# Statistics, banks and closing additions moved in a two-layer graph and mixture-of-experts kernel

## The chip, the cores and the metric

The kernel runs on one core of a Trainium2 chip. The metric is the time of one execution on the device in microseconds; the number that counts is the median of repeated runs. All arithmetic is fp32.

## What is computed

The reference takes 8192 tokens of 128 features (32 graphs of 256 nodes) and passes them through four blocks, each normalised before and added back to the tokens after.

```python
x = x + gated_graph(layernorm(x), adj)      # layer 0: (adj @ x + bias) * gates, relu
x = x + top1_experts(layernorm(x))          # H = gelu(x @ W1 + b1); x = p_e * (H @ Wd[e] + bd[e])
x = x + graph_lstm(layernorm(x), adj)       # layer 1, below
x = x + top2_experts(layernorm(x))          # y_e = (silu(x @ w1_e) * (x @ w3_e)) @ w2_e
```

The third block is

```python
h = relu(einsum('ts,bsh->bth', adj, x @ Wg0 + bg0))
h = relu(einsum('ts,bsh->bth', adj, h @ Wg1 + bg1))
for p in 1..4:                              # windows of p nodes, an LSTM over each
    h[:, last node of each window] = lstm_p(windows of h)
```

## The kernel before

Every engine has its own program, and semaphores tie them. A tile is 128 tokens; there are 64 tiles, held in `X` in on-chip memory through the whole kernel. The order of work on each engine is written out by hand. The stages that matter here are these.

**First experts, b2.** Tokens are sorted by expert into 72 slots, taken four at a time in 18 groups (`NB2`). On TensorE a group is `b2_pe` (hidden products, line 1150, and expert products, line 1291); ScalarE does the gelu; on VectorE `b2_dve` (from line 2016) adds the bias and leaves the result (line 2027), and SyncE stores it. GpSimd gathers the results back in token order (`gather`, line 689) in three runs: tiles 0 to 23, 24 to 31, and 32 to 63. In groups 13 to 16 VectorE also adds eight gathered tiles per group to `X` and takes their statistics (`b3_tile`, line 1991). After group 16 it finishes mean and reciprocal deviation of tiles 0 to 31 together (`b3_finish`, `ln_finish`, lines 1513 to 1532), and at the start of group 17 it normalises the first two groups of four tiles (`g_norm`, line 2006), ahead of the bias of group 17.

**Graph, c1, twice (halves of 32 tiles, eight groups of four).** TensorE per group: `g_mix` (line 1331, into bank 0), `g_hidden` (line 1340), `g_second` (line 1348), `g_out` (line 1359, into bank 3). ScalarE copies the mix out of its bank (`g_mixed`, line 917), and the next mix waits for that copy since both use bank 0. VectorE adds the bias (`g_bias0`, line 2052) and normalises the groups ahead. In the second half, transposes of the first half's result are mixed in (line 1302).

**LSTM, twice.** TensorE lines 1415 and 1422. VectorE adds gathered tiles 32 to 63 during the first one.

**Second experts, d2.** 136 slots (`8 * ND2`), one at a time, in groups of eight. Per slot i: TensorE does the upper products of i (line 1442) and then the lower ones of i - 2 (line 1452, `d2_down`, banks 6 and 7 in turn); ScalarE does silu (line 1032) and copies weights (line 955); VectorE multiplies (line 2243) and scales the result of slot i - 2 into `yd` (`d2_rows_out`, line 2172); GpSimd sends the rows home with an indirect DMA (`rows_home`, line 710). The home rows come back in ten blocks (`D3_BLOCKS`): blocks 0 to 5 of eight tiles, 6 to 9 of four. SyncE loads blocks 0 to 3 (`d3_load(0)`), then 4 and 5 once four additions are done (`d3_load(1)`), stores 0 to 3, stores 4 and 5, and only then loads 6 to 9, for which all rows must be home (line 545), and stores them. Each block needs two additions on VectorE (`d3_add`, line 2193, one per expert). Eight are made within the slots, at those given by `D3_ADDS` counted back from the end (slots 119, 121, ... 133); the four of blocks 4 and 5 and the eight of blocks 6 to 9 follow behind the last slot.

```python
D3_ADDS = (17, 15, 13, 11, 9, 7, 5, 3)
for i in [*D3_OF[1], *D3_OF[2]]:
    for k in range(2):
        d3_add(i, k)
```

Of the kernel before, what the change touches and what calls it, by code (L numbers as in the profile page):

```python
# [5 lines left out]
P = 128  # L6
# [49 lines left out]
def build(nc, x, adj_t, bias_io, gate_w, gate_b, w1, b1, wg, bg, wd, bd, g0_w, g0_b, g1_w, g1_b, wih_t, whh_t, bih, bhh,  # L56
# [4 lines left out]
    MC = N // P  # L61
# [25 lines left out]
    with ExitStack() as ctx:  # L87
# [229 lines left out]
        b3_x, b3_t = sem("b3_x"), sem("b3_t")  # L317
# [34 lines left out]
        D3_ADDS = (17, 15, 13, 11, 9, 7, 5, 3)  # L352
# [229 lines left out]
        def _(pool):  # L582
# [133 lines left out]
            for lo, hi, done in GATHERS:  # L716
                gather(lo, hi, done)
            def t_finish(half, k, n):
                first = half * NGH + n * k
                pool.wait_ge(t_ln, first + n)  # L720
                ln_finish(4 * first, 4 * (first + n), half > 0, t_rstd)
# [28 lines left out]
        def _(act):  # L750
# [166 lines left out]
            def g_mixed(half, i):  # L917
                n = half * NGH + i
                act.wait_ge(c1_ax, n + 1)
                if n >= 2:  # L920
                    act.wait_ge(c1_h, n - 1)
                act.activation(axt[i % 2], bank[0][:, :], ACT.Copy).then_inc(c1_axc, 1)
# [133 lines left out]
        def _(pe):  # L1056
# [267 lines left out]
            def g_mix(half, i):  # L1324
                n = half * NGH + i
                pe.wait_ge(c1_xn, n + 1)
                if n > 0:
                    pe.wait_ge(c1_axc, n)
                for b in range(2):
                    for m in range(MC):  # L1330
                        mm = pe.matmul(bank[0][:, b * N:(b + 1) * N], xn[i % 2][:, MC * b + m, :], adj_sb[:, m, :],  # L1331
# [115 lines left out]
            def d2_down(i, j, expert, straight):  # L1447
# [3 lines left out]
                for c in range(KU):  # L1451
                    mm = pe.matmul(bank[6 + j % 2][:, 0:D], hm[j % 2][0:HC, c * P:(c + 1) * P],  # L1452
# [51 lines left out]
            for j in (6, 7):  # L1504
                d2_down(8 * (ND2 - 1) + j, j, er[j - 6], False)
# [3 lines left out]
        def _(dve):  # L1509
# [491 lines left out]
            def b3_finish(half):  # L2001
                dve.wait_ge(b3_t, (half + 1) * NH)
                ln_finish(half * NH, (half + 1) * NH)


            def g_norm(half, i):
                n = half * NGH + i
                if n >= 2:
                    dve.wait_ge(c1_ax, n - 1)
                for j in range(4):  # L2010
# [5 lines left out]
            def b2_dve(g, k, u, first, last):  # L2016
                if isinstance(g, int) and g == NB2 - 1:
                    g_norm(0, 0)
                    g_norm(0, 1)
# [15 lines left out]
                if ahead_of_end == 2:  # L2035
                    b3_finish(0)
# [88 lines left out]
            for half in range(HALVES):  # L2125
# [25 lines left out]
                for n in range(NL):  # L2151
# [11 lines left out]
                    if half == 0 and n == NL - 3:  # L2163
                        b3_finish(1)


            def d2_rows_out(i):
                g, j = i // 8, i % 8
                dve.wait_ge(d2_y, i + 1)
                if j == 0 and g >= RING:  # L2170
                    dve.wait_ge(d2_out[g % RING], 128 * (g // RING))
                dve.tensor_scalar(yd[g % RING][:, j, :], bank[6 + j % 2][:, 0:D], slot_gate[:, i:i + 1], None,  # L2172
# [92 lines left out]
            for i in [*D3_OF[1], *D3_OF[2]]:  # L2265
# [46 lines left out]
```

## Time and profile before

| | us |
|---|---|
| median of 3 runs | 1147.16 |
| lowest, highest | 1145.66, 1150.82 |
| the profiled execution's own time | 1153.07 |
| its span | 1151.2 |
| TensorE busy in the span | 1024.0 (89%) |
| VectorE busy | 600.0 (52%) |
| ScalarE busy | 619.4 (54%) |
| GpSimd busy | 483.7 (42%) |
| mean granted TensorE clock | 0.956 of full |

The span runs from the first to the last record of one execution; 1.9 us of the execution's own time lie around it. In the rows below the engines are PE (TensorE products), PEld (its weight loads), DVE (VectorE), ACT (ScalarE), POOL (GpSimd) and SP (SyncE, whose queue is SPq). L12 is line 12 of the kernel. An fp32 product is recorded as two passes, so one mix of four products shows as x8. The chain of waits is followed back from the last instruction to what released it.

### The profile page before, as it was taken

The numbers are of one execution on the slowest core, as the hardware profiler recorded it, in microseconds if no ns is written. First come the engines' busy times: TensorE is split into PE (matmuls) and PEld (weight loads), VectorE is DVE, ScalarE is ACT, GpSimd is POOL, SyncE is SP. The second block draws the span as 40 slices with busy tenths as digits, with TensorE's granted clock in tenths as the row PEclk, the third lists the DMA queues.
The fourth block names the chain that finished last, engine by engine and source line by source line (L and its number), as shares of the span: only waits on it lengthen the run. The fifth ranks groups of instructions, "written<-read, shape, count | busy, mean of one in ns | idle before, by whom it ended". The sixth has DMA issues, their size and how long they took to land.

```text
span 1151.2 us, 17554 instructions
## 1 busy us (share of the span) xinstructions
PE 1024.0 (89%) x5432; PEld 715.8 (62%) x5433; DVE 600.0 (52%) x1829; ACT 619.4 (54%) x1158; POOL 483.7 (42%) x703
## 2 busy tenths in 40 slices
PE   5799967899989899999999996999897799989993
PEld 2344423577667544654785463448897798889893
DVE  6977874411174265655756753336464523333365
ACT  4678843444333485655338754456776555545551
POOL 5852274531634420000220075533536666656652
PEclk9899988799998999999999997999998999999997
DMA  9940012232323030000000011121122222212547
GB/s 274 365 193 1 1 50 69 87 97 70 97 71 86 28 116 0 1 1 0 1 1 1 1 48 40 41 61 31 43 62 65 64 81 65 82 62 66 189 164 223
DMA packets 79876, 86.28 MB, mean 75 GB/s; under 512 B 10115, under 2 KB 65971, under 8 KB 79027
## 3 DMA queue, kind: packets, MB, share of 16 engines
q1 hardware_dynamic: 67250, 59.28, 16.2%
q0 software_dynamic: 12544, 25.98, 6.8%
q8 instruction: 44, 0.72, 0.3%
q14 instruction: 38, 0.30, 0.1%
HBM read 40.64 MB, written 44.58 MB: 74 GB/s over the span
## 4 chain that ended last, share of the span: by engine, by line
PE 67%; DVE 13%; ACT 6%; issue 6%; another core or an unknown queue 6%; DMA 1%; ACTq 1%; POOL 1%; DVEq 0%; POOLq 0%; SPq 0%
PE bank L1415 17%; PE bank L1442 14%; PE bank L1422 9%; PE bank L1452 5%; PE bank L1150 4%; PE bank L1291 3%; PE bank L1331 2%; PE bank L1179 2%; PE bank L1359 2%; ACT sb_whh_sb L955 1%; PE bank L1348 1%; PE bank L1320 1%; PE bank L1340 1%; DVE sb_R L1542 1%
## 5 line engine op out<-in xcount | busy, mean ns | idle before, releaser
L1415 PE MATMUL bank<-sb_R,sb_wih_sb 128*128 128x512 f32 (+2 forms) x504 | 203.0, 554 | 15.0 <-ACT sb_R L975 7.6
L975 ACT ACTIVATE sb_R<-bank,sb_lb_sb 128x512 f32<-128x512 f32 (+2 forms) x252 | 153.2, 634 | 93.4 <-PE bank L1422 67.4
L710 POOL DMA_INDIRECT expert_out<-sb_R,sb_slot_row x136 | 132.6, 975 | 115.9 <-ACT sb_R L998 45.5
L2243 DVE TENSOR_TENSOR sb_R<-sb_R,bank 114x384 f32<-114x384 f32 x136 | 75.3, 554 | 181.9 <-ACT sb_R L1032 107.3
L1415 PEld LDWEIGHTS bank<-sb_R,sb_wih_sb 128*128 128x128 f32 x504 | 97.1, 194 | 113.7 <-issue 82.8
L1032 ACT ACTIVATE sb_R<-bank 114x384 f32<-114x384 f32 x136 | 66.4, 489 | 142.5 <-PE bank L1442 102.8
L1442 PE MATMUL bank<-sb_xt,sb_wih_sb 128*114 128x128 f32 x792 | 103.5, 282 | 22.8 <-issue 7.2
L1452 PE MATMUL bank<-sb_BIG,sb_R 114*128 x816 | 115.7, 278 | 0.7 <-DVE sb_R L2172 0.5
L1442 PEld LDWEIGHTS bank<-sb_xt,sb_wih_sb 128*114 128x114 f32 x792 | 94.1, 184 | 28.6 <-issue 25.4
L1422 PE MATMUL bank<-sb_R,sb_whh_sb 128*128 128x512 f32 (+2 forms) x288 | 111.1, 529 | 0.0
L685 POOL DMA_INDIRECT expert_in<-sb_R,sb_dest_i x64 | 64.4, 1007 | 105.1 <-DVE sb_dest_i L1767 62.7
L1452 PEld LDWEIGHTS bank<-sb_BIG,sb_R 114*128 114x128 f32 x816 | 103.5, 194 | 0.9 <-issue 0.9
L1442 PE MATMUL bank<-sb_xt,sb_whh_sb 128*114 128x128 f32 x792 | 98.6, 274 | 5.7 <-ACT sb_wih_sb L955 5.6
L614 POOL TENSOR_TENSOR sb_ln_p<-sb_ST 128x8 f32<-128x8 f32 (+2 forms) x15 | 3.3, 222 | 222.6 <-DVE sb_ST L1657 162.5
L1442 PEld LDWEIGHTS bank<-sb_xt,sb_whh_sb 128*114 128x114 f32 x792 | 91.2, 178 | 8.1 <-issue 7.1
L899 ACT ACTIVATE sb_R<-bank,sb_b_sb 128x512 f32<-128x512 f32 x72 | 47.9, 688 | 83.9 <-PE bank L1150 75.0
L1422 PEld LDWEIGHTS bank<-sb_R,sb_whh_sb 128*128 128x128 f32 x288 | 54.7, 190 | 50.5 <-issue 35.6
L676 POOL DMA_INDIRECT sorted_in<-sb_R,sb_dest_i x64 | 62.9, 983 | 44.2 <-issue 16.9
L729 POOL DMA_INDIRECT expert_in<-sb_R,sb_dest_i x64 | 61.9, 967 | 41.1 <-PE bank L1442 16.2
L1291 PE MATMUL bank<-sb_BIG,sb_R 128*128 x576 | 69.8, 279 | 8.3 <-issue 4.3
L1179 PE MATMUL bank<-sb_xt,sb_w_sb 128*128 128x512 f32 x128 | 68.5, 632 | 9.1 <-ACT sb_R L828 9.1
L1291 PEld LDWEIGHTS bank<-sb_BIG,sb_R 128*128 128x128 f32 x576 | 67.6, 195 | 9.4 <-issue 9.4
(308 smaller groups left out, 1690.9 us busy)
## 6 DMA issues: line engine op xcount, KB each, us to landing
sb_XS<-expert_in SPq DMA_DIRECT2D x17, 528.0 KB
expert_in<-sb_R SPq DMA_DIRECT2D x17, 512.0 KB, 6.1
sb_R<-expert_out SPq DMA_DIRECT2D x6, 1024.0 KB, 8.3
sorted_in<-sb_R SPq DMA_DIRECT2D x9, 512.0 KB, 5.4
sb_XS<-sorted_in SPq DMA_DIRECT2D x18, 256.0 KB
sorted_out<-sb_R SPq DMA_DIRECT2D x18, 256.0 KB
sb_X<-x SPq DMA_DIRECT2D x8, 512.0 KB, 7.4
out<-sb_X SPq DMA_DIRECT2D x6, 512.0 KB
```

Source lines behind the costliest of these rows:

```text
L676: pool.indirect_dma_start(out=sorted_in, out_offset=bass.IndirectOffsetOnAxis(ap=dest_i[:, 0, t:t + 1], axis=0), in_=XN[:, t, :], in_offse ...
L685: pool.indirect_dma_start(out=expert_in, out_offset=bass.IndirectOffsetOnAxis(ap=dest_i[:, k, t:t + 1], axis=0), in_=XR[:, t, :], in_offse ...
L710: pool.indirect_dma_start(out=expert_out, out_offset=bass.IndirectOffsetOnAxis(ap=slot_row[:, i:i + 1], axis=0), in_=yd[i // 8 % RING][:, ...
L975: act.activation(gb[s][k][:, 0:c], bank[4 * s + k][:, 0:c], funcs[k], bias=lb_sb[:, (p - 1) * GATES + k:(p - 1) * GATES + k + 1]).then_inc ...
L1032: act.activation(sl[j % 2][0:HC, :], bank[2 + 2 * (j % 2)][0:HC, 0:KU * P], ACT.Silu).then_inc(d2_silu, 1)
L1179: pe.matmul(bank[2 + c % 2][:, :], w1_sb[:, c * P:(c + 1) * P], xt[b // 2 % 2][:, b % 2 * BANK:(b % 2 + 1) * BANK], start=True, stop=True) ...
L1291: mm = pe.matmul(bank[6 + u][:, j * P:(j + 1) * P], Ht[u][:, c, j * P:(j + 1) * P], wd_sb[:, c, bass.ds(er[j] * D, D)], start=(c == 0 and ...
L1415: mm = pe.matmul(bank[4 * s + k][:, 0:c].rearrange("p (w b) -> p w b", b=GH), wih_sb[:, p - 1, k * P:(k + 1) * P], xin, start=True, stop=( ...
L1422: pe.matmul(bank[4 * s + k][:, 0:c], whh_sb[:, p - 1, k * P:(k + 1) * P], hst[s][:, 0:c], start=False, stop=True).then_inc(l_g, 1)
L1442: mm = pe.matmul(bank[2 + 2 * (j % 2) + part][0:HC, c * P:(c + 1) * P], weights_of(i)[:, part * UP + c * HC:part * UP + (c + 1) * HC], xt[ ...
L1452: mm = pe.matmul(bank[6 + j % 2][:, 0:D], hm[j % 2][0:HC, c * P:(c + 1) * P], down_sb[0:HC, bass.ds(expert * (KU * D) + c * D, D)], start= ...
L2243: dve.tensor_tensor(hm[j % 2][0:HC, :], sl[j % 2][0:HC, :], bank[3 + 2 * (j % 2)][0:HC, 0:KU * P], ALU.mult).then_inc(d2_m, 1)
```

## The change

Four edits. (1) In b2, VectorE finishes the statistics of tiles 0 to 23 after group 15 instead of those of 0 to 31 after group 16, and normalises the first two groups there, ahead of the bias of group 16. (2) The statistics of tiles 24 to 31 are finished by GpSimd, between its second and third run of gathers; the normalisation of the seventh group waits for them. (3) The second mix of each half goes into bank 3 and waits for no copy. (4) `D3_ADDS` holds twelve places, slots 117, 118, 120, 121, 123, 124, 126, 127, 129, 130, 132 and 133, so that only the eight additions of blocks 6 to 9 stand behind the last slot; and the last slot's lower product goes into bank 0 and doesn't wait for the result of slot 133 to be read.

```diff
-        b3_x, b3_t = sem("b3_x"), sem("b3_t")
+        b3_x, b3_t, b3_rstd = sem("b3_x"), sem("b3_t"), sem("b3_rstd")
+        SOON = 3 * NH // 4
+        def mix_bank(i):
+            return bank[3] if i == 1 else bank[0]
-        D3_ADDS = (17, 15, 13, 11, 9, 7, 5, 3)
+        D3_ADDS = (19, 18, 16, 15, 13, 12, 10, 9, 7, 6, 4, 3)
             for lo, hi, done in GATHERS:
                 gather(lo, hi, done)
+                if hi == NH:
+                    pool.wait_ge(b3_t, NH)
+                    ln_finish(SOON, NH, False, b3_rstd)
-                act.activation(axt[i % 2], bank[0][:, :], ACT.Copy).then_inc(c1_axc, 1)
+                act.activation(axt[i % 2], mix_bank(i)[:, :], ACT.Copy).then_inc(c1_axc, 1)
-                if n > 0:
+                if n > 0 and i != 1:
                     pe.wait_ge(c1_axc, n)
-                        mm = pe.matmul(bank[0][:, b * N:(b + 1) * N], xn[i % 2][:, MC * b + m, :], adj_sb[:, m, :],
+                        mm = pe.matmul(mix_bank(i)[:, b * N:(b + 1) * N], xn[i % 2][:, MC * b + m, :], adj_sb[:, m, :],
-            for j in (6, 7):
-                d2_down(8 * (ND2 - 1) + j, j, er[j - 6], False)
+            d2_down(8 * ND2 - 2, 6, er[0], False)
+            d2_down(8 * ND2 - 1, 7, er[1], True, bank[0])
+                if half == 0 and 4 * i == SOON:
+                    dve.wait_ge(b3_rstd, 1)
-                if isinstance(g, int) and g == NB2 - 1:
-                    g_norm(0, 0)
-                    g_norm(0, 1)
-                if ahead_of_end == 2:
-                    b3_finish(0)
+                if ahead_of_end == 3:
+                    dve.wait_ge(b3_t, SOON)
+                    ln_finish(0, SOON)
+                    g_norm(0, 0)
+                    g_norm(0, 1)
-            for i in [*D3_OF[1], *D3_OF[2]]:
+            for i in D3_OF[2]:
                 for k in range(2):
                     d3_add(i, k)
```

## Rows read from the trace of the kernel before

**Rows 1.** The profile's chain of waits, its share of the span by engine

```profile
PE 67%; DVE 13%; ACT 6%; issue 6%; another core or an unknown queue 6%; DMA 1%; ACTq 1%; POOL 1%; DVEq 0%; POOLq 0%; SPq 0%
```

**Rows 2.** Timeline, first graph opening: start, us, engine, line, operation, [idle before it]

```profile
336.88 0.89 DVE L2027 TENSOR_TENSOR sb_R<-bank,sb_BIG 128x128 f32<-128x128 f32 x4
...
341.95 0.22 DVE L1517 TENSOR_TENSOR sb_ln_t<-sb_ST 128x32 f32<-128x32 f32 x1
...
345.33 2.14 DVE L2012 TENSOR_SCALAR sb_xn<-sb_X,sb_MEAN,sb_RSTD 128x128 f32<-128x128 f32 x8
...
346.50 3.08 PE L1331 MATMUL bank<-sb_adj_sb,sb_xn 128*128 128x256 f32 x8 [3.06 <-DVE sb_xn L2012]
347.38 0.89 DVE L2027 TENSOR_TENSOR sb_R<-bank,sb_BIG 128x128 f32<-128x128 f32 x4
...
350.41 3.75 PE L1331 MATMUL bank<-sb_adj_sb,sb_xn 128*128 128x256 f32 x8 [0.84 <-ACT sb_R L922]
...
354.94 1.97 PE L1331 MATMUL bank<-sb_adj_sb,sb_xn 128*128 128x256 f32 x8
```

**Rows 3.** Windows, PE only: stretch, its length, busy (count), granted clock, DMA share

```profile
347.00:347.50 0.50, 0.50 (x3) 0.75 0.00 0
```

**Rows 4.** Timeline and windows, all engines, in b2: an idle TensorE and the clock

```profile
332.60 3.83 PE L1291 MATMUL bank<-sb_BIG,sb_R 128*128 x32 [1.49 <-ACT sb_R L899]
...
330.00:345.00 15.00, 11.94 (x78) 9.24 (x76) 12.47 (x56) 5.66 (x9) 0.67 (x1) 1.00 0.16 45
```

**Rows 5.** Timeline, second graph opening, and one window of PE there

```profile
547.05 1.89 PE L1331 MATMUL bank<-sb_adj_sb,sb_xn 128*128 128x256 f32 x8
...
548.52 1.11 DVE L2012 TENSOR_SCALAR sb_xn<-sb_X,sb_MEAN,sb_RSTD 128x128 f32<-128x128 f32 x4
...
551.00 2.73 PE L1331 MATMUL bank<-sb_adj_sb,sb_xn 128*128 128x256 f32 x8 [2.06 <-ACT sb_R L922]
...
555.48 0.69 DVE L2052 TENSOR_TENSOR sb_R<-bank,sb_bga_sb 128x512 f32<-128x512 f32 x1 [4.22 <-PE bank L1340]
...
552.50:553.00 0.50, 0.50 (x2) 0.50 0.00 0
```

**Rows 6.** Timeline behind the last slot, then two pieces of the chain there

```profile
1132.41 4.87 DVE L2200 TENSOR_TENSOR sb_X<-sb_R,sb_X 128x1024 f32<-128x1024 f32 x4
1132.93 1.53 POOL L710 DMA_INDIRECT expert_out<-sb_R,sb_slot_row  x1 [0.30 <-issue]
...
1143.05 5.40 DVE L2200 TENSOR_TENSOR sb_X<-sb_R,sb_X 128x512 f32<-128x512 f32 x8 [5.77 <-DMA sb_R<-expert_out]
...
1134.76 3.64 DMA expert_out<-sb_R,sb_slot_row
...
1138.65 4.38 DMA sb_R<-expert_out
```

**Rows 7.** Timeline, POOL: first and last of nine statements finishing eight tiles' statistics

```profile
568.51 0.23 POOL L614 TENSOR_TENSOR sb_ln_p<-sb_ST 128x8 f32<-128x8 f32 x1 [5.60 <-DVE sb_ST L1657]
...
570.78 1.67 POOL L623 TENSOR_TENSOR sb_RSTD<-sb_ln_p,sb_minus_half 128x8 f32<-128x8 f32 x1
```

**Rows 8.** Timeline: an addition on DVE and the POOL issue that starts inside it

```profile
1118.72 1.22 DVE L2200 TENSOR_TENSOR sb_X<-sb_R,sb_X 128x1024 f32<-128x1024 f32 x1
...
1119.56 1.21 POOL L710 DMA_INDIRECT expert_out<-sb_R,sb_slot_row  x1 [1.07 <-PE bank L1442]
```

**Rows 9.** Loads of home rows (timeline; landing by the profile's DMA issues), and slot 118

```profile
1082.51 1.94 SPq L556 DMA_DIRECT2D sb_R<-expert_out  x4
...
sb_R<-expert_out SPq DMA_DIRECT2D x6, 1024.0 KB, 8.3
...
1093.32 0.55 DVE L2243 TENSOR_TENSOR sb_R<-sb_R,bank 114x384 f32<-114x384 f32 x1 [1.38 <-remote]
```

**Rows 10.** Timeline: a last indirect DMA with queues quiet, and SP's load released by it

```profile
769.16 0.96 POOL L685 DMA_INDIRECT expert_in<-sb_R,sb_dest_i  x1 [0.30 <-issue]
...
771.45 272.51 SPq L537 DMA_DIRECT2D sb_XS<-expert_in  x15
```

More of the change, by code:

```diff
@@ L1445, in d2_up, with d2_down @@
                 mm.then_inc(d2_h, 1)
-            def d2_down(i, j, expert, straight):
+            def d2_down(i, j, expert, straight, target=None):
+                target = target or bank[6 + j % 2]
                 pe.wait_ge(d2_m, i + 1)
@@ L1451, in d2_down @@
                 for c in range(KU):
-                    mm = pe.matmul(bank[6 + j % 2][:, 0:D], hm[j % 2][0:HC, c * P:(c + 1) * P],
+                    mm = pe.matmul(target[:, 0:D], hm[j % 2][0:HC, c * P:(c + 1) * P],
                                    down_sb[0:HC, bass.ds(expert * (KU * D) + c * D, D)],
@@ L1999, in b3_tile, with b3_finish @@
                         dve.bn_stats(ST[:, q, :], X[:, q, :]).then_inc(b3_t, 1)
-            def b3_finish(half):
-                dve.wait_ge(b3_t, (half + 1) * NH)
-                ln_finish(half * NH, (half + 1) * NH)
+            def b3_finish():
+                dve.wait_ge(b3_t, 2 * NH)
+                ln_finish(NH, 2 * NH)
             def g_norm(half, i):
@@ L2163, in _ @@
                     if half == 0 and n == NL - 3:
-                        b3_finish(1)
+                        b3_finish()
             def d2_rows_out(i):
                 g, j = i // 8, i % 8
+                source = bank[0] if i == 8 * ND2 - 1 else bank[6 + j % 2]
                 dve.wait_ge(d2_y, i + 1)
@@ L2171, in d2_rows_out @@
                     dve.wait_ge(d2_out[g % RING], 128 * (g // RING))
-                dve.tensor_scalar(yd[g % RING][:, j, :], bank[6 + j % 2][:, 0:D], slot_gate[:, i:i + 1], None,
+                dve.tensor_scalar(yd[g % RING][:, j, :], source[:, 0:D], slot_gate[:, i:i + 1], None,
                                   ALU.mult).then_inc(d2_yo, 1)
```

## The prediction

> **What bounds the kernel now.** I read the chain of waits first, to see which engine's time is the kernel's time: TensorE holds 67% of it [rows 1]. So an edit pays only where TensorE waits, or behind its last product. Then I read the timeline at the three places that the change touches.
>
> In the first graph opening TensorE ends the last expert product at 343.44 (346.50 less 3.06 idle) and waits for VectorE, which finishes the statistics from 341.95 to 345.33 and then normalises. The first two mixes take 3.08 and 3.75 us where the third takes 1.97 [rows 2]. The reason is the granted clock: it goes from full to half, 2.4 to 1.2 GHz, inside the window at 347.0 to 347.5, after TensorE had stood idle for 3.06 us [rows 3]. An idle of 1.49 us in the group before left the clock at 1.00 [rows 4]. In the second opening the first mix ends at 548.94 and the second starts at 551.00, after the copy out of bank 0; it takes 2.73 us, and the window at 552.5 shows 0.50 [rows 5]. Behind the last slot the chain goes through GpSimd's last row transfer (3.64 us to landing), the first load of home rows (4.38) and eight additions (5.40) [rows 6].
>
> **The change part by part.**
>
> **Statistics a group sooner.** VectorE's work is only put in another order. From 336.88: statistics 3.38 us (341.95 to 345.33) and two normalisations of 2.05 (345.33 to 347.38), so the first normalised group is there at 341.3 and the second at 342.3, both before TensorE ends at 343.44. The bias of group 16 slips from 336.88 to 342.3; its eight tiles (4.18 us, from 337.77 to 341.95) end at 347.4, and the bias of group 17 starts at 347.4 as before [rows 2]. Narrower statistics (24 columns for 32) may give back 0.1 us. TensorE then mixes at full clock: 343.5 to 345.4, the second until 347.3, the first hidden product (354.16 to 354.94 in [rows 2], 0.8 us) until 348.1. The third mix needs the third normalisation, which stands behind group 17's bias: 347.4 + 0.9 + 1.1 = 349.4. Before it started at 354.94. Gain 5.5 us; what is late next is this third normalisation, with an idle of 1.3 us before it, shorter than the 1.49 of [rows 4] that left the clock alone.
> Moved with it: the store of group 16's result on SyncE goes 5.4 us later, but the third run of gathers needs the store of group 17, which doesn't move. The expert product of group 17 needs only the bias of group 15. I put both at nothing.
>
> **Last eight tiles by GpSimd.** Nine statements, 568.51 to 572.45, so 3.9 us [rows 7]. They start once the tiles are added (347.4) and end at 351.3. Behind them on GpSimd stand the 32 gathers of tiles 32 to 63, each of which also waits for a hidden product (the first at 348.1) and for the last store. They lose at most 3.2 us, and their readers are in the LSTM after eight graph groups. The seventh normalisation waits for the fifth mix, thus until after 349.5 + 3 x 1.9 = 355.2; the cover is 3.9 us. Cost nothing; without that cover TensorE would wait for the rest.
>
> **Second mix in its own bank.** In the first half it is worth nothing, since the third mix waits for VectorE anyway: with the copy's 0.84 us of wait [rows 2] the hidden product would end at 348.9, still before 349.4. In the second half the second mix is held only by its normalisation, which ends at 549.63. It runs until 551.5, the hidden product until 552.3, and VectorE's bias, at 555.48 before, starts at 552.4 [rows 5]. That is 2.06 - 0.7 of wait and the rest half clock: TensorE's idle shrinks to 0.7 us. Gain 3.1. Bank 3 is next written by the first output product, two rounds later, behind the copy.
>
> **Twelve additions within the slots.** An addition of 1.22 us [rows 8] is put where VectorE waits 1.38 us, as before slot 118's product [rows 9]; two slots in three take one, where before one in two did. A slot lasts 2.3 us (slot 118's product at 1093.32, slot 129's addition at 1118.72, [rows 8, 9]), and VectorE's own work in one is 0.55 us of product and a scaling that I take as no longer, so 2.3 with an addition. Behind an addition a product can slip a little, and the slot without one takes it up. TensorE wants the product only two slots later: nothing, bounds -0.5 and +1.5 us, since GpSimd and VectorE may each be held by the other once. The first addition wants block 0 at 1091.9 (1093.32 - 1.38); the load was issued at 1082.51 and takes 8.3, so it is there at 1090.8 [rows 9]. Loads 4 and 5 and all stores of 0 to 5 go out some 9 us earlier on SyncE, since the fourth addition comes at slot 121 instead of 125.
> Behind the last slot four additions of 1.22 us vanish, but not from the end: they run from 1132.41 to 1137.28, and the loads of blocks 6 to 9 wait until 1138.4 for the last rows [rows 6]. What goes is what they did to others. (a) An indirect DMA issued inside an addition is held: it starts at 1119.56, the addition ends at 1119.94, it ends at 1120.77, 0.83 us later [rows 8]. The same sum gives the 1.53 us at 1132.93 (addition ends 1133.63). Without it 0.96: gain 0.57. (b) Two stores of 512 KB stand before the last transfer: 3.64 us to landing, against 2.29 with quiet queues (769.16 to 771.45) [rows 6, 10]: gain 1.35, bounds 0 and 1.35. (c) The first load shares the queues with the end of the last store: between 0 and 2.1 (4.38 less 2.29); I take 0.7, half of what a block of that size takes (5.40 over 4) [rows 6, 10]. The eight last additions stay. Together 2.6, bounds 0 and 4.0.
> The Trainium skill ("SBUF — State Buffer", section "Who interferes with whom") says that a VectorE instruction with two inputs on chip blocks a GpSimd instruction that reads there, not one that only writes, and infers that tensor_tensor therefore doesn't hold descriptor generation. By that rule term (a) is nothing and the sum 0.6 us smaller; the trace disagrees, with 1.21 and 1.53 against 0.96, and I go by the trace.
>
> **The last slot's bank.** GpSimd issues rows one after another (0.96 and 0.30 between), and the last was issued at 1134.76 while its rows were scaled before the additions began at 1132.41 [rows 6]. The queue is GpSimd's: nothing.
>
> **Sum.** 5.5 + 3.1 + 2.6 = 11.2 us. The profiled execution took 1153.07 (span 1151.2 and 1.9 around it), so its like would take 1141.9. It stands 5.9 above the median; from the median 1147.16 - 11.2 = 1136.0.
>
> **The rivals.**
> *The tail gives nothing:* landing is bound by the transfer and not by its company, and the loads take what they took. For it: one quiet landing is thin evidence. 1136.0 + 2.6 = 1138.6. A case within it, with 0.04 of its chance: the row issue is slow for another reason than the addition, so only (a) fails: 1136.6. The rule of the Trainium skill above would give this.
> *The clock falls in the first opening all the same.* TensorE is idle for 1.3 us where 2.06 and 3.06 came before a fall and 1.49 didn't. The first two mixes took 6.8 us together where two at full clock take 3.8 [rows 2]; of these 3.0 us 1.3 would lie in the idle: 1136.0 + 1.7 = 1137.7.
> *Both openings fall to half clock and the tail gives nothing:* 1.7 in the first, 1.8 in the second (551.00 to 555.48 is 4.5 us for a mix and a hidden product that take 1.9 and 0.8 [rows 5]): 11.2 - 2.6 - 3.5 = 5.1, thus 1142.1, within 0.5%.
> *Slower:* the additions wait for their blocks. Place: slot 117, where block 0 has 1.1 us to spare by 8.3 us of landing. VectorE stands still, then TensorE, since the upper product of slot i needs the multiplied slot i - 2. It decides once VectorE waits over 11.2 us in all at these twelve places, and passes 0.5% at 17; block 4, loaded at slot 121 and wanted at 129, has 8 x 2.3 - 8.3 = 10 us to spare on top, so a single late block doesn't do it. With 18 us of waiting 1154. Against it: before, the only wait in front of an addition is the 5.77 us behind the last slot [rows 6].
>
> **How the numbers follow.** A measurement of this kernel can tell about 0.5% (5.7 us) from no change. Chances: forecast 0.52, tail nothing 0.16, clock in the first opening 0.14, both 0.12, slower 0.04, and 0.02 for something that gives all back. Faster 0.82, same 0.14, slower 0.04. The forecast's own bounds are 1134.5 (tail 4.0) to 1138; with the scatter of the median (1.5 below, 3.7 above in three runs) and the case of both falls the range is 1132.0 to 1142.5.
>
> **What would show it.** The first mix starts right behind the last expert product, with no idle before it, and the third about 6 us after it; granted clock 1.00 in both openings; nine GpSimd statements between gathers; the second mix of the second half starts 0.7 us after the first ends; no 1.53 us row issue behind the last slot; about 2.3 us from the last issue to the loads; no VectorE idle before its additions in the slots. A half clock in an opening, an idle at slot 117, or a landing of 3.6 us would show the step that failed.

## The result and the profile after

Six runs of each kernel on one chip: 1146.37 us before (1145.66 to 1150.82), 1139.64 after (1137.37 to 1141.25), ratio 0.9931 with an interval of 0.9916 to 0.9945. By the ratio that is 7.9 us less (6.3 to 9.6). The two medians themselves lie 6.7 us apart, inside that interval; ratio and median are two estimates from the same runs, and every "us less" below goes by the ratio. The forecast was 1136.0 with a range of 1132.0 to 1142.5 and "faster" at 0.82: sign and range hold, and the measured time is 3.6 us longer than forecast. One run of the kernel before on the second chip below (1237.6 us) and one of e5_fill there (2109.5 us) stand far above all others and are in no ratio. The profiled pair differs by more than the medians: 1153.07 against 1141.25, 11.8 us (spans 1151.2 and 1139.5). That is close to the forecast sum of 11.2. Why a pair of profiles shows the sum and the medians don't is the main question below.

The timeline of the kernel after, first opening, beside [rows 2] (start, us, engine, line, operation, [idle before it]):

```profile
343.14 0.87 DVE L2034 TENSOR_TENSOR sb_R<-bank,sb_BIG 128x128 f32<-128x128 f32 x4
...
344.33 3.62 PE L1338 MATMUL bank<-sb_adj_sb,sb_xn 128*128 128x256 f32 x16
...
347.66 1.08 ACT L929 ACTIVATE sb_R<-bank 128x512 f32<-128x512 f32 x2 [6.02 <-DVE sb_X L2002]
...
348.24 0.21 POOL L618 TENSOR_TENSOR sb_ln_p<-sb_ST 128x8 f32<-128x8 f32 x1 [16.52 <-DVE sb_ST L2007]
348.26 0.88 DVE L2034 TENSOR_TENSOR sb_R<-bank,sb_BIG 128x128 f32<-128x128 f32 x4
...
348.31 1.12 PE L1347 MATMUL bank<-sb_R,sb_g_sb 128*128 128x512 f32 x2 [0.37 <-ACT sb_R L929]
...
349.06 1.10 DVE L2022 TENSOR_SCALAR sb_xn<-sb_X,sb_MEAN,sb_RSTD 128x128 f32<-128x128 f32 x4
...
350.21 1.99 PE L1338 MATMUL bank<-sb_adj_sb,sb_xn 128*128 128x256 f32 x8 [0.78 <-DVE sb_xn L2022]
...
350.38 1.67 POOL L627 TENSOR_TENSOR sb_RSTD<-sb_ln_p,sb_minus_half 128x8 f32<-128x8 f32 x1
...
352.71 1.08 POOL L708 DMA_INDIRECT sb_R<-sorted_out,sb_dest_i  x1 [0.59 <-POOL sb_pause_p L663]
```

The reader is to see three things. The sixteen products of the first two mixes stand as one group of 3.62 us with no idle before it, where before there were 3.08 and 3.75 us after 3.06 of idle. The third mix comes 5.9 us after the last expert product (344.33 to 350.21) where it came 11.5 after (343.44 to 354.94), and its idle of 0.78 us is VectorE's third normalisation, behind the bias of group 17. And one line that the prediction doesn't have: ScalarE's first copy of a mix starts at 347.66, 1.4 us after the first mix ends (344.33 and 1.89 us for a mix), released by VectorE's sums (L2002) and not by TensorE. GpSimd's nine statements run from 348.24 to 352.05; the gather behind them starts at 352.71.

The second opening, beside [rows 5]:

```profile
543.67 1.89 PE L1338 MATMUL bank<-sb_adj_sb,sb_xn 128*128 128x256 f32 x8
...
546.28 1.99 PE L1338 MATMUL bank<-sb_adj_sb,sb_xn 128*128 128x256 f32 x8 [0.72 <-DVE sb_xn L2022]
...
549.17 0.69 DVE L2062 TENSOR_TENSOR sb_R<-bank,sb_bga_sb 128x512 f32<-128x512 f32 x1 [1.32 <-PE bank L1347]
...
549.87 1.89 PE L1338 MATMUL bank<-sb_adj_sb,sb_xn 128*128 128x256 f32 x8
```

The idle is 0.72 us for 2.06, the mix takes 1.99 us for 2.73, and from the first mix to the third it is 6.2 us. Before, the third mix started at 556.24, 9.19 us after the first.

The granted clock over the two openings, from the first mix to the third (stretch, length, busy of PE, PEld, DVE, ACT, POOL, clock, DMA share, GB/s):

```profile
344.30:350.30 6.00, 4.86 (x21) 3.26 (x19) 5.75 (x24) 1.08 (x2) 1.69 (x8) 1.00 0.19 53
543.60:549.90 6.30, 5.58 (x28) 4.26 (x27) 4.95 (x14) 2.61 (x6) 0.00 (x0) 1.00 0.00 0
```

It is full (2.4 GHz) in both, where [rows 3] and [rows 5] have 0.75 and 0.50.

Behind the first opening the kernel after gives some of this back, at a place that the prediction doesn't look at:

```profile
365.61 1.06 ACT L940 ACTIVATE sb_R<-bank 128x512 f32<-128x512 f32 x1 [4.08 <-remote]
...
367.14 1.16 PE L1355 MATMUL bank<-sb_g_sb,sb_R 128*128 128x128 f32 x8 [1.04 <-ACT sb_R L936]
```

ScalarE waits 4.08 us for something that the profile can't name ("remote"), and TensorE then waits 1.04 us for ScalarE. The sixth and the seventh mix start 6.5 us apart, where they are 5.2 us apart in the kernel before.

In the slots and behind the last one, beside [rows 6, 8], first the timeline, then two pieces of the chain:

```profile
1083.40 1.22 DVE L2211 TENSOR_TENSOR sb_X<-sb_R,sb_X 128x1024 f32<-128x1024 f32 x1
...
1083.46 1.98 POOL L714 DMA_INDIRECT expert_out<-sb_R,sb_slot_row  x1 [0.30 <-issue]
...
1115.68 1.22 DVE L2211 TENSOR_TENSOR sb_X<-sb_R,sb_X 128x1024 f32<-128x1024 f32 x1
...
1116.52 1.20 POOL L714 DMA_INDIRECT expert_out<-sb_R,sb_slot_row  x1 [0.92 <-PE bank L1449]
...
1123.72 0.96 POOL L714 DMA_INDIRECT expert_out<-sb_R,sb_slot_row  x1 [0.31 <-issue]
...
1131.42 5.40 DVE L2211 TENSOR_TENSOR sb_X<-sb_R,sb_X 128x512 f32<-128x512 f32 x8 [8.50 <-DMA sb_R<-expert_out]
...
1124.98 2.22 DMA expert_out<-sb_R,sb_slot_row
...
1127.45 3.94 DMA sb_R<-expert_out
```

The last row issue but one takes 0.96 us where it took 1.53, the last rows land in 2.22 where it was 3.64, the first load takes 3.94 where it was 4.38: 0.57 + 1.42 + 0.44 = 2.4 us. The additions now stand inside the slots, none of the twelve with an idle before it. Each row issue that starts inside one ends 0.82 to 0.84 us after it (1084.62 and 1085.44, 1116.90 and 1117.72), so these issues take 1.01 to 1.98 us. An issue that had started before the addition isn't held: it takes 0.95 or 0.96 us, as outside.

One line of the kernel before belongs beside the landing, how long SyncE itself waited for it (us in total, times, longest):

```profile
SPq L545 <- DMA expert_out<-sb_R,sb_slot_row: 0.7, 1, 0.7
```

SyncE came to this wait only 0.7 us before the rows had landed, since it stood in the store of block 5, which waits for the fourth addition. So a sooner landing alone would have been worth 0.7 us at most; it is worth 1.42 because the additions moved, and SyncE's wait for them with them.

### The profile page after: what moved, and what is told of

Same layout as the page of the kernel before. It is cut to its first block, busy times and chain, and to the rows that moved or that the text cites. A ratio compares the mean times of both kernels' runs of the same rounds, so it can differ in the third digit from the quotient of the medians.

```text
span 1139.5 us, 17561 instructions
## 1 busy us (share of the span) xinstructions
PE 1016.3 (89%) x5432; PEld 712.0 (62%) x5433; DVE 599.0 (53%) x1829; ACT 618.5 (54%) x1158; POOL 489.1 (43%) x712
## 4 chain that ended last, share of the span: by engine, by line
PE 67%; DVE 13%; another core or an unknown queue 7%; ACT 6%; issue 4%; ACTq 1%; DMA 1%; POOL 0%; DVEq 0%; POOLq 0%; SPq 0%
PE bank L1422 16%; PE bank L1449 15%; PE bank L1429 9%; PE bank L1460 5%; PE bank L1157 4%; PE bank L1298 4%; PE bank L1186 2%; PE bank L1366 2%; ACT sb_whh_sb L962 1%; PE bank L1338 1%; ACTq L956 1%; PE bank L1327 1%; PE bank L1355 1%; DVE sb_R L1550 1%
## 5 line engine op out<-in xcount | busy, mean ns | idle before, releaser
L1422 PE MATMUL bank<-sb_R,sb_wih_sb 128*128 128x512 f32 (+2 forms) x504 | 200.2, 548 | 14.5 <-ACT sb_R L982 10.6
```

The lines of the kernel that those rows point to most:

```text
L1422: mm = pe.matmul(bank[4 * s + k][:, 0:c].rearrange("p (w b) -> p w b", b=GH), wih_sb[:, p - 1, k * P:(k + 1) * P], xin, start=True, stop=( ...
```

## The experiments

They ran on two other chips than the pair above. On the second one the kernel before takes 1158.3 and 1158.7 us in two series (27 runs between 1150.5 and 1162.7; 27 between 1150.1 and 1162.1). On the third it takes 1063.7 (9 runs, 1061.5 to 1064.3). Microseconds behind a ratio are the ratio times the median of before there.

To compare the traces I measure five stretches in each:

- O1, the first opening: from the end of the last expert product (the first mix's start less its idle) to the third mix of the first half;
- R, the rest of that half: from its third mix to the first mix of the second half;
- O2, the second opening: from the first mix to the third of the second half;
- D, in the expert slots: from the first to the last upper product whose weights lie in `sb_wih_sb`. Slots take `sb_wih_sb` and `sb_whh_sb` in turn, two slots each, so this last product is not that of the last slot, which comes 3.9 us later;
- T, the tail: from the end of D to the end of the span.

In brackets: the edits of this stretch that the kernel has ("part" is the statistics without GpSimd).

```
                 chip    O1 us          R us            O2 us          D us    T us
before           first   11.5           192.1           9.2            335.2   26.1
after            first    5.9 (all)     193.5 (stats)   6.2 (bank)     335.7   23.6 (adds)
e1_stats         second   6.9 (stats)   193.3 (stats)   9.2            340.4   26.2
e2_bank          second  10.6 (bank)    192.6           6.2 (bank)     342.4   26.0
e3_adds          second   8.6           192.6           9.2            339.4   23.7 (adds)
e5_fill          second   8.8 (fill)    192.2           7.5 (fill)     340.7   25.8
e6_whole         second   5.9 (all)     193.7 (stats)   6.2 (bank)     338.9   23.6 (adds)
e8_third         second   4.4 (all)     196.0 (stats)   6.2 (bank)     340.3   23.7 (adds)
e9_dve           second   9.4 (part)    194.6 (part)    6.2 (bank)     340.1   23.6 (adds)
e10_order        second  10.0           192.6           7.5            339.2   27.5 (order)
e4_same          third   11.2           192.1           7.5            290.1   26.0
e12_same         third   10.0           192.1           7.5            290.1   25.8
e15_half1        third    5.5 (stats)   192.1 (stats)   6.2 (bank)     290.1   23.6 (adds)
e14_last         third    4.4 (all)     192.1 (stats)   6.2 (bank)     290.1   23.7 (adds)
```

R holds what O1 alone would hide. On the third chip it is 192.1 us whatever the kernel. On the first two it is 192.1 to 192.6 with the old order of the statistics and 193.3 to 196.0 with the new one, so about 1 us of the gain in the first opening is given back there, and more in e8_third and e9_dve. In e6_whole and e1_stats it goes where it went in the kernel after, between the sixth and the seventh mix (6.7 and 6.4 us apart). GpSimd's eight tiles aren't the cause, since e9_dve has none of them and an R of 194.6; what ScalarE and VectorE wait for there stays open.

Between the openings and the slots, from the third mix of the second half to the first product of D, lies a stretch that no kernel here edits. It takes 225.3 to 233.7 us on the first two chips and 214.5 to 214.6 on the third. So single executions on the first two chips can differ there by more than the whole change is worth.

### The three parts alone: e1_stats, e2_bank, e3_adds

e1_stats is the kernel before with the order of VectorE's statistics and GpSimd's last eight tiles changed, and no other edit.

```diff
-                if ahead_of_end == 2:
-                    b3_finish(0)
+                if ahead_of_end == 3:
+                    dve.wait_ge(b3_t, SOON)
+                    ln_finish(0, SOON)
+                    g_norm(0, 0)
+                    g_norm(0, 1)
...
```

> Only the statistics are moved (tiles 0 to 23 a group sooner, the last eight tiles on GpSimd). Theory A (the forecast's terms hold in every execution): 5.5 us faster than before, ratio 0.9952, and no half clock in the first opening. Theory B (the profiled execution of before lost more in its openings and slots than its timed runs do, so each term is worth less in timed runs): 2 to 4 us, ratio 0.9965 to 0.998. In the profile of either the third mix starts some 6 us after the last expert product ends.

Measured: 1153.99 us, ratio 0.9947 (0.9926 to 0.9968), 6.1 us less (3.7 to 8.6), as theory A had it. O1 is 6.9 us, not some 6. Its timeline there:

```profile
346.16 1.89 PE L1335 MATMUL bank<-sb_adj_sb,sb_xn 128*128 128x256 f32 x8
...
350.26 1.97 PE L1335 MATMUL bank<-sb_adj_sb,sb_xn 128*128 128x256 f32 x8 [2.21 <-ACT sb_R L926]
```

The second mix waits 2.21 us for ScalarE's copy out of bank 0, not the 0.84 of [rows 2]. That copy stands behind ScalarE's wait for all 32 sums of the first half, which in the kernel before had long been met, and now has not. So in the first half the second bank isn't worth nothing once the statistics are sooner: it takes 1.0 us more off (6.9 to 5.9).

e2_bank is the kernel before with the second mix of each half in bank 3.

```diff
-                if n > 0:
+                if n > 0 and i != 1:
                     pe.wait_ge(c1_axc, n)
-                        mm = pe.matmul(bank[0][:, b * N:(b + 1) * N], ...
+                        mm = pe.matmul(bank[3 if i == 1 else 0][:, b * N:(b + 1) * N], ...
...
```

> Only the second mix gets its own bank. In the first opening the second mix then follows the first without the copy's 0.84 us, still behind the late statistics. Theory A: 3.1 us in the second opening and up to 1 us in the first, together 3 to 4 us, ratio 0.9965 to 0.997. Theory B: 1.5 to 2.5 us, only the idle without the clock.

Measured: 1153.99 us, 0.9965 (0.9942 to 0.9988), 4.1 us less (1.4 to 6.7), again theory A's figure. In the trace O2 is 6.2, as forecast. In O1 the clock fell as in the kernel before:

```profile
348.44 6.76 PE L1331 MATMUL bank<-sb_adj_sb,sb_xn 128*128 128x256 f32 x16 [3.05 <-DVE sb_xn L2012]
```

Two mixes in 6.76 us; alone they take 3.62 at full clock in the kernel after.

e3_adds moves the twelve additions and nothing else.

```diff
-        D3_ADDS = (17, 15, 13, 11, 9, 7, 5, 3)
+        D3_ADDS = (19, 18, 16, 15, 13, 12, 10, 9, 7, 6, 4, 3)
-            for i in [*D3_OF[1], *D3_OF[2]]:
+            for i in D3_OF[2]:
```

> Only the twelve additions within the slots. Theory A: 2.6 us from the tail, ratio 0.9977, landing of the last rows 2.3 us instead of 3.64 in the profile. Theory B: the tail gives the same 2.5 us but the denser additions cost 1 to 3 us in the slots, so the ratio is 0.999 to 1.0.

Measured: 1155.09 us, 0.9968 (0.9943 to 0.9993), 3.7 us less (0.8 to 6.6), over theory A's 2.6 and against theory B. T is 23.7, 2.4 below the kernel before. But this trace has more in it, in a place that it doesn't edit, the first opening:

```profile
348.01 1.99 PE L1331 MATMUL bank<-sb_adj_sb,sb_xn 128*128 128x256 f32 x8 [3.06 <-DVE sb_xn L2012]
...
350.84 1.97 PE L1331 MATMUL bank<-sb_adj_sb,sb_xn 128*128 128x256 f32 x8 [0.84 <-ACT sb_R L922]
...
346.00:348.00 2.00, 0.00 (x0) 0.00 (x0) 1.86 (x9) 0.00 (x0) 0.00 (x0) 1.00 0.00 0
348.00:350.00 2.00, 1.99 (x8) 1.44 (x8) 1.78 (x8) 0.00 (x0) 0.00 (x0) 1.00 0.00 0
350.00:352.00 2.00, 1.16 (x7) 1.06 (x7) 1.12 (x4) 0.60 (x1) 0.00 (x0) 1.00 0.49 127
```

The same code, the same idle of 3.06 us to the hundredth, and the clock stays at 1.00: 1.99 and 1.97 us for mixes that took 3.08 and 3.75 in [rows 2]. So a fall after this idle is something that happens in some executions and not in others.

### Filling the idle: e5_fill

The kernel before, with products that nobody reads in TensorE's two idles, into bank 2, which is free there; each is 128x512 and stands as two records.

```diff
+                if (half, i) == (0, 0):
+                    fill(3)
+                if (half, i) == (1, 1):
+                    fill(2)
...
```

> The kernel before, with TensorE kept busy by idle products into a bank that nobody reads: three ahead of the first mix of the first half and two ahead of the second mix of the second half (2.6 and 1.7 us at full clock, into idle times of 3.06 and 2.06). If half clock costs what the profile shows in every execution (theory A): 3.0 + 1.7 = 4.7 us faster less nothing, ratio 0.996. If timed runs mostly keep the clock (theory B): no change, ratio 1.000 within 0.001.

Measured: 1155.32 us, 0.9961 (0.9938 to 0.9984), so 4.5 us less (1.9 to 7.2) by work that is thrown away. That is theory A's 0.996, and the interval leaves out theory B's 1.000. Of "in every execution" it shows less: the trace of e3_adds is an execution in which the first opening had no half clock to lose, and an interval 5 us wide can't tell "always" from "often". The waits for VectorE and ScalarE are still there; O1 is 8.8 and O2 7.5:

```profile
548.42 1.88 PE L1326 MATMUL bank<-sb_w_sb,sb_ident 128*128 128x512 f32 x4
550.64 1.97 PE L1339 MATMUL bank<-sb_adj_sb,sb_xn 128*128 128x256 f32 x8 [0.34 <-ACT sb_R L922]
```

The second mix of the second half takes 1.97 us where it took 2.73, and starts where it did, 3.9 us after the first. This splits the forecast term of 3.1 us there: 1.7 us is clock (9.2 to 7.5), 1.3 is the wait itself (7.5 to 6.2). In the first opening it is 2.7 (11.5 to 8.8) and 2.9 (8.8 to 5.9).

### The kernel before again: e4_same and e12_same

> The kernel before, unedited, for its trace. Theory (after a given idle TensorE's clock falls in some executions and not in others): of the two openings at least one differs from the first profile of before, where both were at half clock: 8.6 to 11.5 us from the last expert product to the third mix, 7.5 or 9.2 from the first to the third mix of the second half. Rival (the fall belongs to the kernel, and the other profiles differ by their edits): 11.5 and 9.2 again.

> The kernel before, unedited, a second time, for its trace. Theory (the clock falls in some executions and not in others): the two openings take 8.6 to 11.5 us and 7.5 or 9.2, not as in the other unedited execution in every place. Rival (the fall belongs to the kernel): 11.5 and 9.2 again.

Two unedited executions on the third chip, 1064.23 and 1062.84 us. The first opening of e4_same, then of e12_same:

```profile
323.64 2.60 PE L1331 MATMUL bank<-sb_adj_sb,sb_xn 128*128 128x256 f32 x8 [2.76 <-DVE sb_xn L2012]
327.08 3.75 PE L1331 MATMUL bank<-sb_adj_sb,sb_xn 128*128 128x256 f32 x8 [0.84 <-ACT sb_R L922]
```

```profile
323.41 3.68 PE L1331 MATMUL bank<-sb_adj_sb,sb_xn 128*128 128x256 f32 x8 [2.75 <-DVE sb_xn L2012]
327.93 1.97 PE L1331 MATMUL bank<-sb_adj_sb,sb_xn 128*128 128x256 f32 x8 [0.84 <-ACT sb_R L922]
...
526.74 1.97 PE L1331 MATMUL bank<-sb_adj_sb,sb_xn 128*128 128x256 f32 x8 [2.06 <-ACT sb_R L922]
```

After the same idle the fall begins at another moment: it takes in the end of one mix and all of the other in the first, one mix only in the second. O1 is 11.2 and 10.0. In the second opening neither fell (1.97 us, O2 7.5) after the 2.06 us that stand before the fall in [rows 5]. The theory holds, the rival falls (it wanted 11.5 and 9.2 again). Over the unedited openings in all traces: O1 fell in 4 of 5 (before, e4_same, e12_same, e10_order; not e3_adds), once fully, once nearly so and twice for one mix; O2 fell in 3 of 6 (before, e1_stats, e3_adds). In e2_bank, whose edit comes behind that idle, O1 fell too. None fell where the idle is filled or is 1.1 us or less, nor in e1_stats after 2.21 us. On the second chip the 27 runs of before have a mean granted clock of 0.960 and e5_fill's eleven 0.963; within the 27 a run is 0.95 us shorter for each 0.001 of clock, though that correlation is loose (-0.58).

### The whole on the second chip: e6_whole

> The whole change once more, on the chip on which other kernels of this call run. Forecast's terms (5.5 + 3.1 + 2.6): 11.2 us less than before, ratio 0.990, in every execution. Rival (the clock falls in the first opening of before only in some executions, so that the term there is 5.6 us in these and 2.8 in the others): 8 to 11 us less, 0.991 to 0.993. In its profile both expect granted clock 1.00 through the first opening, the third mix 5.9 us after the last expert product, and in the second 6.2 us from first to third mix.

Measured: 1150.07 us, 0.9934 (0.9903 to 0.9964), 7.6 us less (4.2 to 11.2), the ratio of the first chip once more. The forecast's 0.990 lies at the edge of the interval, the rival's 0.991 to 0.993 within it. O1, R, O2 and T are those of the kernel after (5.9, 193.7, 6.2, 23.6). The three parts alone add up to 13.9 us against 7.6. They share one series of before, in which runs lie 12 us apart, so its error is in the sum three times; the traces give no sign of parts that work against each other. That this is all of the difference isn't shown.

An estimate from the stretches of this chip: O1 of the unedited openings is 9.3 on average (8.6 and 10.0) and becomes 5.9, O2 8.6 (9.2, 9.2 and 7.5) and becomes 6.2, T falls by 2.4 and R grows by 1.2 (192.5 to 193.7). That is 3.4 + 2.4 + 2.4 - 1.2 = 7.0 us, beside 7.6 timed. It rests on two and three executions.

### What is left of the first opening: e8_third and e9_dve

e8_third takes two waits out of the kernel after: ScalarE's wait for the sums, and the third normalisation behind group 17.

```diff
-                act.wait_ge(b3_x, (half + 1) * NH)
+                if half > 0:
+                    act.wait_ge(b3_x, 2 * NH)
...
                         b3_tile(t)
+                        if t == SOON + 3:
+                            g_norm(0, 2)
...
```

> The changed kernel, with ScalarE's wait for all 32 sums before its first copy of a mix taken away in the first half (it reads no sums) and the third normalisation moved before the last four tiles of group 16. In the changed kernel the third mix starts 5.9 us after the last expert product: the first two take 3.6, the copy that the second hidden product needs stands behind ScalarE's wait, and the third normalisation stands behind the bias of group 17. Theory (these two waits are what is left of the opening): the third mix starts 4.6 to 5.0 us after the last expert product, and the kernel takes 1.0 us less than the changed one (0.2 more of a per cent against before). Rival (VectorE is the bound of the opening, so what is pulled forward is missing behind it): the third mix is sooner but the fourth waits for its normalisation, and the eighth starts when it did: 0 us.

Measured: 1150.62 us, 0.9931 (0.9906 to 0.9957), beside 0.9934 for e6_whole. Its timeline:

```profile
346.98 3.62 PE L1339 MATMUL bank<-sb_adj_sb,sb_xn 128*128 128x256 f32 x16
...
351.38 1.97 PE L1339 MATMUL bank<-sb_adj_sb,sb_xn 128*128 128x256 f32 x8
354.41 1.16 PE L1356 MATMUL bank<-sb_g_sb,sb_R 128*128 128x128 f32 x8 [1.06 <-ACT sb_R L936]
...
356.26 1.89 PE L1339 MATMUL bank<-sb_adj_sb,sb_xn 128*128 128x256 f32 x8
```

The third mix comes 4.4 us after the first (5.9 in e6_whole), but the product behind it waits 1.06 us for ScalarE's relu, which waits for VectorE's bias. The fourth mix comes 9.3 us after the first, in e6_whole 9.5. So the wait mostly moves one product on, and behind the opening R is 2.4 us longer than in e6_whole (196.0 and 193.7), more than the 1.5 won in O1. The rival had the result, 0 us; its reason, that VectorE is the bound, is seen at this one product and not shown for the rest.

e9_dve gives the last eight tiles' statistics back to VectorE.

```diff
-                if hi == NH:
-                    pool.wait_ge(b3_t, NH)
-                    ln_finish(SOON, NH, False, b3_rstd)
+                if ahead_of_end == 2:
+                    dve.wait_ge(b3_t, NH)
+                    ln_finish(SOON, NH)
...
```

> The changed kernel, with the statistics of the last eight tiles by VectorE, behind the tiles of group 16, and none by GpSimd. Theory (VectorE's order sets the third mix, GpSimd's nine statements are covered): the statistics take some 3.1 us whatever the number of columns, the third mix starts 3.1 us later, at 9 us after the last expert product, TensorE stands idle for 3.9 us before it and the clock falls: 3.1 to 4.8 us more than the changed kernel, which gives back half of the edit on the first opening. Rival (GpSimd's statements delay the gathers behind them and so cost in the LSTM what they save here): 0 to 1 us more.

Measured: 1155.31 us, 0.9971 (0.9949 to 0.9994): 3.4 us less than before where e6_whole was 7.6 less; the difference of the ratios, 0.0037, is 4.3 us, inside the 3.1 to 4.8 expected. The two intervals overlap (0.9903 to 0.9964 and 0.9949 to 0.9994), so here the trace is the better witness: O1 is 3.5 us longer than in e6_whole and R 0.9.

```profile
355.95 3.78 PE L1335 MATMUL bank<-sb_adj_sb,sb_xn 128*128 128x256 f32 x8 [4.22 <-DVE sb_xn L2017]
...
354.00:356.00 2.00, 0.05 (x1) 0.05 (x1) 2.00 (x9) 0.00 (x0) 0.00 (x0) 0.52 0.08 25
```

TensorE stands idle for 4.22 us, the clock falls to 0.52, and the third mix comes at 9.4 us. Statistics a group sooner are worth little by themselves; it needs GpSimd for the last eight tiles, which the forecast had rightly at no cost.

### The tail: e10_order and e14_last

e10_order is the kernel before with the loads of blocks 6 to 9 ahead of the stores of blocks 4 and 5 on SyncE.

```diff
             d3_store(0)
-            d3_store(1)
             d3_load(2)
+            d3_store(1)
             d3_store(2)
```

> The kernel before, with one exchange in SyncE's order: the loads of blocks 6 to 9 stand before the stores of blocks 4 and 5; all additions stay where they were. Theory (terms b and c of the forecast: the two stores slow the last row transfer and the first load): from the last row issue to the first load 2.2 to 2.3 us where it was 3.64, the load 3.9 or less where it was 4.38, the last row issue still 1.5 us because the addition holds it: 1.8 us less than before, ratio 0.998. Rival (the landing was long for another reason, such as the held issue, or the stores now slow the last loads or stand before the last stores): 0 us or slower.

Measured: 1160.13 us, 1.0020 (0.9994 to 1.0046): no gain, as the rival had it. In its trace (timeline of GpSimd and VectorE, then two pieces of the chain):

```profile
1135.69 1.68 POOL L710 DMA_INDIRECT expert_out<-sb_R,sb_slot_row  x1 [0.30 <-DVE sb_R L2172]
...
1144.17 2.75 DVE L2200 TENSOR_TENSOR sb_X<-sb_R,sb_X 128x512 f32<-128x512 f32 x4 [3.99 <-DMA sb_R<-expert_out]
1147.29 2.94 DVE L2200 TENSOR_TENSOR sb_X<-sb_R,sb_X 128x512 f32<-128x512 f32 x4 [0.37 <-DMA sb_R<-expert_out]
...
1137.67 2.23 DMA expert_out<-sb_R,sb_slot_row
...
1141.48 7.31 DMA sb_R<-expert_out
```

This parts the three terms of the tail. The additions are where they were, and the row issue is still held (1.68 us). The stores are gone from the landing's company, and it takes 2.23 us for 3.64. So (a) belongs to the addition and (b) to the two stores. Term (c) has no run of its own: the first load takes 4.1 to 4.4 us in five of the six traces with an unedited tail (in the sixth, e1_stats, the chain goes through a later load of 5.4) and 3.8 to 4.0 in the seven with the edited one, so the 0.44 of the profiled pair is one draw. T as a whole is steadier, 25.8 to 26.2 us in the six and 23.6 to 23.7 in the seven. In e10_order, though, the stores only stand elsewhere: they share the queues with the last loads, the last of which takes 7.31 us, and T is 27.5, 1.4 longer than before. Only an earlier addition lets the stores leave early; another order alone is worth nothing or less.

e14_last puts the last slot's lower product back into bank 7, behind the scaling.

```diff
-            d2_down(8 * ND2 - 1, 7, er[1], True, bank[0])
+            d2_down(8 * ND2 - 1, 7, er[1], False)
...
```

> The changed kernel, with the last slot's lower product back in bank 7, behind the scaling of the rows two slots earlier. Forecast (the rows are scaled before GpSimd, which issues them one after another, comes to them): 0 us, the last row issue and its landing where they were. Rival (the lower product's wait for VectorE is on the path to the last issue): 0.3 to 0.6 us more between the last upper product and the last row issue, which in the changed kernel are 9.1 us apart.

Measured on the third chip: 1053.13 us, 0.9907 (0.9894 to 0.9921), 9.9 us less than before (8.4 to 11.3). From the end of D to the last row issue it is 9.1 us, as in the kernel after. The forecast of 0 holds. This run is the whole change but for an edit without effect, on the chip whose runs scatter least:

```profile
319.89 3.62 PE L1338 MATMUL bank<-sb_adj_sb,sb_xn 128*128 128x256 f32 x16
...
324.29 1.97 PE L1338 MATMUL bank<-sb_adj_sb,sb_xn 128*128 128x256 f32 x8
```

No product waits in its first opening. Its stretches against e4_same and e12_same: O1 5.6 to 6.8 us less, O2 1.3, R and D the same to 0.1 us, T 2.1 to 2.3; together 9.0 to 10.4, and 9.9 was timed.

### The bank in the first half: e15_half1

```diff
-            return bank[3] if i == 1 else bank[0]
+            return bank[3] if (half, i) == (1, 1) else bank[0]
...
```

> The changed kernel, with the second mix's own bank in the second half only; in the first half it goes to bank 0, behind the copy. Forecast (there the own bank is worth nothing, as the third mix waits for VectorE): the third mix still 5.9 us after the last expert product, 0 us. Theory (ScalarE's first copy waits for all 32 sums, so the copy out of bank 0 ends late and the second mix behind it): the second mix waits about 2.2 us for the copy, the third mix comes 6.9 us after the last expert product, 1.0 us more; too little for the timed ratio to tell, so the trace decides.

Measured: 1054.33 us, 0.9921 (0.9907 to 0.9934); the intervals of this and e14_last meet. O1 is 5.5 against 4.4:

```profile
320.51 1.89 PE L1338 MATMUL bank<-sb_adj_sb,sb_xn 128*128 128x256 f32 x8
323.24 1.96 PE L1338 MATMUL bank<-sb_adj_sb,sb_xn 128*128 128x256 f32 x8 [0.84 <-ACT sb_R L929]
```

The 1.0 us that the theory gave is there (1.1), but not by its mechanism: the wait is 0.84 us for the plain copy, not 2.2. On this chip VectorE is further ahead (the second normalisation ends 3.7 us before the first mix, at 316.8; on the first chip 1.1 us before, at 343.2), so ScalarE's wait for the sums is already met. The third mix there doesn't wait for VectorE either, and thus every microsecond of the copy counts.

## Why the prediction was right, and where it wasn't

**The sum was made against an execution in which the clock fell in full at both places.** That is the step that was mis-sized: the half-clock part of the terms 5.5 and 3.1. The forecast took 1153.07 less 11.2 and carried the 11.2 over to the median. Against that execution each term was right: 5.6 in the first opening (5.5 forecast), 3.0 in the second (3.1), 2.4 to 2.5 in the tail (2.6), together 11.0 us. But where the clock doesn't fall, the first opening gives 2.8 (8.6 to 5.9 between two chips) and the second 1.3, and the sum is 6.5.

**A term that the forecast put at nothing.** R is 1.4 us longer in the kernel after (192.1 to 193.5), and the prediction has no term for it. With it the sum on the first chip is 9.6 us where the clock falls in full and 5.1 where it stays, and 7.9 us were timed, between the two. The estimates of the other chips come out near what was timed: 7.0 for 7.6 on the second, 9.0 to 10.4 for 9.9 on the third, where R doesn't grow. That timed runs are such a mixture is worked out from traces; the timed runs don't show the clock of an opening by itself. How often it falls on the first chip was not tried.

**Partly luck.** That the profiled pair differs by 11.8 us, so near to 11.2, isn't all of the forecast's making. Beside the 11.0 of its terms the two executions differ by +1.4 in R, +0.9 before the first opening, +0.5 in D and -3.3 in the unedited stretch between the openings and the slots. The forecast had a rival for the clock falling in the kernel after, and none for its not falling in the kernel before. The same profile could have warned of it: it stood 5.9 us over the median.

**Statistics sooner.** The mixes start behind the last expert product at full clock, as forecast. Missed: ScalarE's wait for the sums, which was met early before and became late with the new order, and its price of 1.0 us without the own bank. The third mix came at 5.9 us, as forecast, with an idle of 0.78 us instead of 1.3.

**GpSimd's eight tiles.** No wait for them, as forecast, 3.8 us of statements for 3.9, and necessary: without them O1 is 3.5 us longer, and 4.3 us are lost by the ratios.

**Second bank.** Second half right in the profile, 1.3 of its 3.1 us there in each trace and 1.7 hanging on the clock. First half wrong: 1.0 to 1.1 us, not 0. In the kernel after the two errors hide each other, since the 5.5 were given to the statistics alone.

**Additions in the slots.** Nothing, as forecast: D is 290.1 us in all four traces of the third chip, with and without them. No addition waited for its block, so the slower rival had nothing to stand on.

**The tail.** 2.4 to 2.5 of 2.6 us. (a) 0.57 for 0.57, (b) 1.42 for 1.35, (c) 0.44 for 0.7. What (b) left out is that SyncE was held by the fourth addition until 0.7 us before the landing. "SBUF — State Buffer", section "Who interferes with whom", of the Trainium skill infers that tensor_tensor doesn't hold the making of descriptors; the trace disagrees again, in the kernel after with 1.01 to 1.98 us for row issues that start inside an addition against 0.95 outside, and in e10_order with 1.68 where only the stores were moved. Which part of the issue is held, the making of descriptors or the reading of its row numbers from on-chip memory, no run here tells.

**The rivals.** The first two gave 1138.6 and 1137.7, nearer to 1139.64 than the forecast, and neither happened: the tail gave its 2.4 and the clock in both openings of the kernel after stayed at 1.00. A time alone would have picked the wrong cause.

## What to carry to other kernels

Before an idle of TensorE is priced with the half clock behind it, ask whether every execution pays that: one profile shows one draw, and a profile that stands well above the median of its runs has probably drawn badly. Split such a term into the wait, which goes in each execution, and the clock, which goes only where it fell. Then follow the trace past the edited place: what an opening wins can be given back 20 us later. And when an engine's work is pulled forward, list every wait on other engines that was satisfied early by the old order; they come due next.

## What was not expected of the hardware

- TensorE's clock after the same idle of the same code fell in some executions and not in others: after 3.06 us in the kernel before, not in e3_adds; after 2.06 us in three of six. Where it fell, it began at different moments. The Trainium skill ("TensorE: Matmul & The Clock Gate", Part 1) calls the number of slow products at a kernel's start run-variable; these traces agree in kind, and show it for a fall in the middle of a kernel.
- Products that nobody reads made the kernel before 4.5 us (1.9 to 7.2) faster.
- A row issue by GpSimd that starts inside a VectorE addition of 1.22 us ends 0.82 to 0.84 us behind it; one that started before the addition takes 0.95 us, as outside.
- The same kernel took 1147, 1158 and 1064 us on three chips. The chain of waits names part of the difference. First the kernel before on the first chip, whose row is in [rows 1], has 6% for another core or an unknown queue and 6% for issue; on the third chip it has

```profile
PE 80%; DVE 11%; ACT 3%; DMA 2%; issue 2%; POOL 1%; ACTq 0%; DVEq 0%; POOLq 0%; SPq 0%
```

  with 2% of issue and nothing unknown. Stretch D takes 290.1 us there in each of four traces and 335 to 342 on the others. What holds the engines there was not tried.
